# W^T V of a low-rank feed-forward kernel, taken row by row of W, with all loads on SP's queue

## The chip, the cores and the metric

One core of one Trainium2 chip runs the whole program. The metric is device time in microseconds of one execution: 156.87 us, the median of three runs (156.59 to 157.31). TensorE, VectorE, ScalarE, GpSimd and SyncE stand in the profile as PE, DVE, ACT, POOL and SP.

## What is computed

The input x is 2048 tokens (32 x 64) of 1024 numbers. With W 1024 x 1024, eight low-rank experts A (16 x 1024 each) and B (1024 x 16 each), a router Wr (8 x 1024), U (1024 x 256), S (256) and V (1024 x 256):

```
logits = x Wr^T + 5 * onehot(id of the row)         two best experts per token
gates  = softmax of the two best logits
c      = x W^T + 2 * sum_e gate_e * (x A_e^T) B_e^T
out    = x + (c V) * S U^T                          (U * S) V^T applied to c
```

All is fp32. The kernel never forms c: it builds P = W^T V (1024 x 256) once, so that c V = x P + the gated expert part times (B^T V), and multiplies every tile of x by A, Wr and P together.

## The kernel before

**Precision.** Every fp32 operand of a product is split into a high part, rounded to fp32r by a copy on ACT, and a low part, operand minus high part, computed on DVE (for x on POOL). A product is then three matmuls, hi x hi, hi x lo and lo x hi (`triple`, lines 316 to 319).

**The first stage: P = W^T V.** The contraction runs over the 1024 rows of W and V, in eight groups k of 128 rows. The rows of W are loaded in two halves of 512 columns: the first half lies in `vw_raw` beside the 256 columns of V (one transfer of 384 KB for each k), the second half in `w_raw` (one of 256 KB for each k). The stage has sixteen chunks i, one half of W for one k each. Chunk i needs `w_hi` and `w_lo` (a ring of four) and `v_hi`, `v_lo` of its k. On PE a chunk is four column groups of 128 times three matmuls of 256 columns, twelve matmuls (`p_chunk`, line 348); the first is written out in `p_first`. The order before is all eight k of the first half (chunks 0 to 7), then all eight k of the second half (chunks 8 to 15). The eight column groups of P accumulate in four PSUM banks `fin`: banks 0 and 1 are finished after chunk 7, banks 2 and 3 after chunk 15. `split_p` copies a finished bank into `proj_hi` (ACT) and `proj_lo` (DVE).

**What else passes through ACT and DVE in this stage,** in program order, which each engine keeps: the split of A and Wr (`aw_raw`, ACT line 665, DVE line 880) after chunk 12, the split of the first tile of x (ACT line 571, then POOL line 273) after chunk 13, the high part of B (ACT line 673) after chunk 14, and `split_p` of banks 0 and 1 after chunk 11. A wait in one of these holds all that stands behind it on the same engine. `split_w` on ACT waits for the load, and for chunk i - 4 on PE because of the ring.

**Loads.** ACT's queue issues the W parts (all but the first 128 columns) of the first three transfers of V and W; SP's queue issues everything else: the other parts of these three, five whole transfers of V and W, the ids, the eight second halves of W, then A with Wr, the first tile of x transposed, B, the second tile, S, U, and more of x.

**After the stage,** `step(s)` runs over the sixteen tiles of 128 tokens: 24 matmuls of 392 columns on PE for a tile (`project`, line 359), routing on DVE and ACT, and the products with U for pairs of tiles. `step(0)` waits for A, Wr, the first tile and the finished banks of P.

Of the kernel before, what the change touches and what calls it, by code (L numbers as in the profile page):

```python
# [16 lines left out]
def adaln_ffn(nc, xt, x, ids, VW, W, AW, B, U, S, out):  # L17
    P = 128
# [26 lines left out]
    with ExitStack() as ctx:  # L45
# [65 lines left out]
        bv_ps = zt[:, RANK:2 * RANK]  # L111

        vw_load = [sem(f"vw_load{k}") for k in range(OC)]
        vw_rest_load = [sem(f"vw_rest_load{k}") for k in range(3)]
        w_load = [sem(f"w_load{k}") for k in range(OC)]
        aw_load = sem("aw_load")
        b_load = sem("b_load")
# [16 lines left out]
        aw_lo = sem("aw_lo")  # L134
        b_hi_done = sem("b_hi_done")
        b_lo_done = sem("b_lo_done")
        p_hi = sem("p_hi")
        p_lo = sem("p_lo")
        us_hi_done = sem("us_hi_done")
# [42 lines left out]
        bank_a, bank_b, bank_c, bank_d = fin  # L182

        def w_chunk(i):
            return vw_raw[:, i, RANK:RANK + HQ] if i < OC else w_raw[:, i - OC, :]

        block = ctx.enter_context(nc.Block())

# [1 line left out]
        @block.sync  # L190
        def _(sp):
            def load_w(k):
                sp.dma_start(w_raw[:, k, :], W[k, :, :]).then_inc(w_load[k], 16)

            def load_xt(t):
                if t >= XTR:
                    sp.wait_ge(xt_lo, t - XTR + 1)
                sp.dma_start(xt_raw[:, t % XTR, :, :], xt[t, :, :, :]).then_inc(xt_load[t % XTR], 16)

            def load_x(t):  # L200
                if t >= XR:
                    sp.wait_ge(stored[t % XR], 16 * (t // XR))
                sp.dma_start(x_all[:, t % XR, :], x_v[t, :, :]).then_inc(x_load[t % XR], 16)

            def store_head(t):
                sp.wait_ge(end_read, HALF * t + HALF)
                sp.dma_start(out_v[t, :, :], x_all[:, t % XR, :]).then_inc(stored[t % XR], 16)

            def store_pair(p):
                sp.wait_ge(fin_read, READS * (p - 1) + 6)  # L210
                sp.dma_start(out_v[2 * p, :, :], x_all[:, (2 * p) % XR, :]).then_inc(stored[(2 * p) % XR], 16)
                sp.wait_ge(side_add, ADDS * (p - 1) + 3)
                sp.dma_start(out_v[2 * p + 1, :, :], x_all[:, (2 * p + 1) % XR, :]).then_inc(stored[(2 * p + 1) % XR], 16)

            first = RANK + P
            for k in range(3):
                sp.dma_start(vw_raw[:, k, 0:first], VW[k, :, 0:first]).then_inc(vw_load[k], 16)
            for k in range(3, OC):
                sp.dma_start(vw_raw[:, k, :], VW[k, :, :]).then_inc(vw_load[k], 16)
            sp.dma_start(ids_i[:, :], ids).then_inc(ids_load, 16)  # L220
            for k in range(OC):
                load_w(k)
            sp.dma_start(aw_raw[:, :, :], AW).then_inc(aw_load, 16)
            load_xt(0)
            sp.dma_start(b_raw[:, :, :], B).then_inc(b_load, 16)
            load_xt(1)
            sp.dma_start(s_col[:, :], S).then_inc(s_load, 16)
            sp.dma_start(u_raw[:, :, :], U).then_inc(u_load, 16)
            for t in range(2, XTR):
                load_xt(t)  # L230
            for t in range(XR):
                load_x(t)
            for s in range(TILES):
                if s + XTR < TILES:
                    load_xt(s + XTR)
                if s >= 6 and s % 2 == 0:
                    load_x(s)
                    load_x(s + 1)
                if s in (4, 5):
                    store_head(s - 4)  # L240
                if s >= 7 and s % 2 == 1:
                    store_pair((s - 5) // 2)
            p = PAIRS - 2
            sp.wait_ge(fin_read, READS * (p - 1) + 4)
            sp.dma_start(out_v[2 * p, :, 0:BANK], x_all[:, (2 * p) % XR, 0:BANK]).then_inc(stored[(2 * p) % XR], 16)
            sp.wait_ge(fin_read, READS * (p - 1) + 5)
            sp.wait_ge(side_add, ADDS * (p - 1) + 3)
            sp.dma_start(out_v[2 * p + 1, :, :], x_all[:, (2 * p + 1) % XR, :]).then_inc(stored[(2 * p + 1) % XR], 16)
            sp.wait_ge(fin_read, READS * (p - 1) + 6)
            sp.dma_start(out_v[2 * p, :, BANK:D], x_all[:, (2 * p) % XR, BANK:D]).then_inc(stored[(2 * p) % XR], 16)  # L250
            for n in range(5):
                t, lo, hi = ((LAST - 1, 0, BANK), (LAST - 1, BANK, D), (LAST, 0, BANK),
                             (LAST, BANK, BANK + BANK // 2), (LAST, BANK + BANK // 2, D))[n]
                sp.wait_ge(end_read, HEAD_PRODS + n + 1)
                sp.dma_start(out_v[t, :, lo:hi], x_all[:, t % XR, lo:hi]).then_inc(stored[t % XR], 16)
            for j in range(XR):
                n = len(range(j, TILES, XR)) + (2 if j == LAST % XR else 1 if j in ((LAST - 1) % XR, (LAST - 3) % XR) else 0)
                sp.wait_ge(stored[j], 16 * n)
# [56 lines left out]
        def _(pe):  # L315
# [30 lines left out]
                last.then_inc(w_used, 1)  # L346

            def p_chunk(i):
                h, k = divmod(i, OC)
                pe.wait_ge(w_lo_done, i + 1)  # L350
                if h == 0:
                    pe.wait_ge(v_lo_done, k + 1)
                for m in range(MH):
                    cols = slice(m * P, (m + 1) * P)
                    last = triple(p_dst(h, m), w_hi[:, i % WRING, cols], w_lo[:, i % WRING, cols],
                                  v_hi[:, k, :], v_lo[:, k, :], False, True, shared=True)
                last.then_inc(w_used, 1)

            def project(t, k):
                q = t % 2  # L360
# [101 lines left out]
            def step(s, gh_at=1, mix_at=4, z_later=False):  # L462
# [3 lines left out]
                for k in range(DC):  # L466
                    if s == 0 and k == 0:
                        pe.wait_ge(aw_lo, 1)
                        pe.wait_ge(p_lo, 2)
                    if s == 0 and k in (MH, MH + 2):  # L470
                        pe.wait_ge(p_lo, k // 2 + 1)
                    last = project(s, k)
                    if s >= 1 and k == gh_at:
# [68 lines left out]
        @block.scalar  # L542
        def _(act):
            def split_w(i):
                h, k = divmod(i, OC)
                if i == 0:
                    act.wait_ge(vw_rest_load[0], 16)
                    nc.scalar.copy(w_hi[:, 0, P:HQ], w_chunk(0)[:, P:HQ]).then_inc(w_hi_done, 1)
                    return
                if i in (1, 2):  # L550
                    act.wait_ge(vw_rest_load[i], 16)
                if i >= OC:
                    act.wait_ge(w_load[i - OC], 16)
                if i >= WRING:
                    act.wait_ge(w_used, i - WRING + 1)
                nc.scalar.copy(w_hi[:, i % WRING, :], w_chunk(i)).then_inc(w_hi_done, 1)  # L556
# [3 lines left out]
                nc.scalar.copy(v_hi[:, k, :], vw_raw[:, k, 0:RANK]).then_inc(v_hi_done, 1)  # L560

            def split_p(b):
                act.wait_ge(w_used, OC if b < 2 else 2 * OC)
                nc.scalar.copy(proj_hi[:, 2 * b:2 * b + 2, Z0:COLS],
                               fin[b][:, :].rearrange("p (c n) -> p c n", c=2)).then_inc(p_hi, 1)

# [83 lines left out]
                    if s + 2 < TILES:  # L650
                        split_x(s + 2)

            first = RANK + P
            for k in range(3):
                act.dma_start(vw_raw[:, k, first:], VW[k, :, first:]).then_inc(vw_rest_load[k], 16)  # L655
            act.wait_ge(const, 3 + E)
            nc.scalar.activation(esum[:, :], iota_e[:, 0:1], ACT.Exp).then_inc(act_warm, 1)
            act.wait_ge(act_warm, 1)
            for i in range(2 * OC):
                if i < OC:  # L660
                    split_v(i)
                split_w(i)
                if i == OC + 4:
                    act.wait_ge(aw_load, 16)
                    nc.scalar.copy(proj_hi[:, :, 0:Z0], aw_raw[:, :, :]).then_inc(aw_hi, 1)
                if i == OC + 3:
                    split_p(0)
                    split_p(1)
                if i == OC + 5:
                    split_x(0)  # L670
                if i == OC + 6:
                    act.wait_ge(b_load, 16)
                    nc.scalar.copy(b_hi[:, :, :], b_raw[:, :, :]).then_inc(b_hi_done, 1)
            split_p(2)
            split_p(3)
            split_x(1)
            exp_top(0)
            split_x(2)
# [18 lines left out]
        def _(dve):  # L697
# [172 lines left out]
            dve.wait_ge(vw_load[0], 16)  # L870
            nc.vector.tensor_copy(w_hi[:, 0, 0:P], w_chunk(0)[:, 0:P]).then_inc(w_first_hi, 1)
            for i in range(2 * OC):
                if i < OC:
                    split_v(i)
                split_w(i)
                if i == OC:
                    make_target()
                if i == OC + 4:
                    dve.wait_ge(aw_hi, 1)
                    nc.vector.tensor_sub(proj_lo[:, :, 0:Z0], aw_raw[:, :, :],  # L880
                                         proj_hi[:, :, 0:Z0].bitcast(F32)).then_inc(aw_lo, 1)
                if i == OC + 3:
                    split_p(0)
                    split_p(1)
            split_p(2)
            split_p(3)
            dve.wait_ge(b_hi_done, 1)
            nc.vector.tensor_sub(b_lo[:, :, :], b_raw[:, :, :], b_hi[:, :, :].bitcast(F32)).then_inc(b_lo_done, 1)
            dve.wait_ge(setup, 2)
# [66 lines left out]
```

## Time and profile before

| what | value |
|---|---|
| median of three runs | 156.87 us |
| the profiled execution's own time | 156.68 us |
| its span on the core | 154.9 us |
| PE busy | 150.1 us, 97% of the span |
| DVE, POOL, ACT busy | 103.1, 70.1, 65.1 us |
| granted TensorE clock, mean | 1.0 of full speed |
| mean DMA rate over the span | 211 GB/s |

Times in the profile count from the start of the span. A busy figure says how long an engine executed something, not that the end hangs on it. What decides an edit is what each instruction waited for in the stretch that the edit touches; the listing in order of time, read for each engine, shows that.

### The profile page before, as it was taken

The numbers are of one execution on the slowest core, as the hardware profiler recorded it, in microseconds if no ns is written. First come the engines' busy times: TensorE is split into PE (matmuls) and PEld (weight loads), VectorE is DVE, ScalarE is ACT, GpSimd is POOL, SyncE is SP. The second block draws the span as 40 slices with busy tenths as digits, with TensorE's granted clock in tenths as the row PEclk, the third lists the DMA queues.
The fourth block names the chain that finished last, engine by engine and source line by source line (L and its number), as shares of the span: only waits on it lengthen the run. The fifth ranks groups of instructions, "written<-read, shape, count | busy, mean of one in ns | idle before, by whom it ended". The sixth has DMA issues, their size and how long they took to land.

```text
span 154.9 us, 2559 instructions
## 1 busy us (share of the span) xinstructions
PE 150.1 (97%) x883; PEld 139.8 (90%) x883; DVE 103.1 (67%) x299; ACT 65.1 (42%) x147; POOL 70.1 (45%) x53
## 2 busy tenths in 40 slices
PE   7899999999999999999999999999999999999991
PEld 5799999999998999989998999899999989998880
DVE  0698697353658798765578476929692967396861
ACT  4696692519724642551155125414441642233200
POOL 2000024087764741259445935591669068701800
PEclk9999999999999999999999999999999999999999
DMA  5999999995303064148428744854680087006184
GB/s 184 326 395 395 405 418 405 408 402 204 135 7 130 4 271 135 80 154 310 136 99 312 268 135 180 287 215 135 261 259 25 0 292 252 2 22 253 70 333 141
DMA packets 10957, 32.72 MB, mean 211 GB/s; under 512 B 1472, under 2 KB 2496, under 8 KB 10816
## 3 DMA queue, kind: packets, MB, share of 16 engines
q1 hardware_dynamic: 10512, 31.96, 55.9%
q10 hardware_dynamic: 432, 0.59, 1.1%
q8 instruction: 7, 0.11, 0.3%
q14 instruction: 6, 0.05, 0.1%
HBM read 24.16 MB, written 8.39 MB: 210 GB/s over the span
## 4 chain that ended last, share of the span: by engine, by line
PE 93%; DMA 3%; DVE 1%; ACT 0%; ACTq 0%; issue 0%; DVEq 0%
PE pj L317 16%; PE pj L318 16%; PE pj L319 16%; PE fin L317 14%; PE fin L318 13%; PE fin L319 13%; DMA vw_raw<-in_VW 3%; PE zt L384 2%; PE gt L366 1%; PE zt L317 1%; PE zt L319 1%; PE zt L318 1%; DVE w_lo L702 0%; ACT w_hi L556 0%; DVE x_all L831 0%; ACTq L655 0%
## 5 line engine op out<-in xcount | busy, mean ns | idle before, releaser
L273 POOL TENSOR_TENSOR xT_lo<-xt_raw,xT_hi 128x1024 fp32r<-128x1024 f32 x16 | 40.5, 2532 | 55.1 <-ACT xT_hi L571 55.1
L317 PE MATMUL pj<-proj_hi,xT_hi 128*128 128x392 f32 x128 | 44.9, 351 | 0.0
L318 PE MATMUL pj<-proj_lo,xT_hi 128*128 128x392 f32 x128 | 43.5, 340 | 0.0
L319 PE MATMUL pj<-proj_hi,xT_lo 128*128 128x392 f32 x128 | 43.5, 340 | 0.0
L288 POOL TENSOR_TENSOR x_all<-x_all,vw_raw 128x512 f32<-128x512 f32 x18 | 23.0, 1295 | 17.5 <-DVE vw_raw L806 17.5
L317 PE MATMUL fin<-v_hi,w_hi 128*128 128x256 f32 (+1 forms) x84 | 26.9, 321 | 0.5 <-DVE w_lo L702 0.5
L318 PE MATMUL fin<-v_lo,w_hi 128*128 128x256 f32 (+1 forms) x84 | 26.3, 313 | 0.0
L319 PE MATMUL fin<-v_hi,w_lo 128*128 128x256 f32 (+1 forms) x84 | 26.3, 313 | 0.0
L317 PEld LDWEIGHTS pj<-proj_hi,xT_hi 128*128 128x128 f32 x128 | 24.0, 188 | 1.0
L318 PEld LDWEIGHTS pj<-proj_lo,xT_hi 128*128 128x128 f32 x128 | 24.1, 188 | 0.5
L319 PEld LDWEIGHTS pj<-proj_hi,xT_lo 128*128 128x128 f32 x128 | 24.0, 188 | 0.0
L734 DVE SCALAR_TENSOR_TENSOR logit<-target,pj 128x8 f32<-128x8 f32 x16 | 2.6, 161 | 23.3 <-PE pj L319 23.3
L317 PEld LDWEIGHTS fin<-v_hi,w_hi 128*128 128x128 f32 x84 | 16.0, 190 | 1.7 <-DVE w_lo L702 0.9
L319 PEld LDWEIGHTS fin<-v_hi,w_lo 128*128 128x128 f32 x84 | 16.0, 190 | 0.9
L571 ACT CAST xT_hi<-xt_raw 128x1024 fp32r<-128x1024 f32 x16 | 16.8, 1047 | 0.0
L318 PEld LDWEIGHTS fin<-v_lo,w_hi 128*128 128x128 f32 x84 | 16.0, 191 | 0.7
L812 DVE TENSOR_TENSOR x_all<-fin,x_all 128x512 f32<-128x512 f32 x24 | 15.3, 681 | 0.0
L317 PE MATMUL fin<-us_hi,w_hi 128*128 128x512 f32 (+1 forms) x36 | 14.8, 410 | 0.0
L617 ACT CAST ghT_hi<-gt 128x128 fp32r<-128x128 f32 x16 | 4.3, 267 | 22.7 <-PE gt L366 22.7
L319 PE MATMUL fin<-us_hi,w_lo 128*128 128x512 f32 (+1 forms) x36 | 13.7, 380 | 0.0
L318 PE MATMUL fin<-us_lo,w_hi 128*128 128x512 f32 (+1 forms) x36 | 13.7, 380 | 0.0
L625 ACT ACTIVATE etop<-dtop 128x2 f32<-128x2 f32 x16 | 3.3, 203 | 20.9 <-DVE dtop L739 20.9
(87 smaller groups left out, 230.8 us busy)
## 6 DMA issues: line engine op xcount, KB each, us to landing
xt_raw<-in_xt SPq DMA_DIRECT2D x16, 512.0 KB, 3.6
x_all<-in_x SPq DMA_DIRECT2D x16, 512.0 KB, 5.7
out<-x_all SPq DMA_DIRECT2D x13, 512.0 KB, 2.7
w_raw<-in_W SPq DMA_DIRECT2D x8, 256.0 KB, 7.3
vw_raw<-in_VW SPq DMA_DIRECT2D x5, 384.0 KB, 6.8
out<-x_all SPq DMA_DIRECT2D x5, 256.0 KB, 2.0
u_raw<-in_U SPq DMA_DIRECT2D x1, 1024.0 KB, 13.0
vw_raw<-in_VW SPq DMA_DIRECT2D x3, 192.0 KB, 3.3
```

What stands on the lines that cost most here:

```text
L273: nc.gpsimd.tensor_sub(xT_lo[:, t % 2, :, :], xt_raw[:, t % XTR, :, :], xT_hi[:, t % 2, :, :].bitcast(F32)).then_inc(xt_lo, 1)
L288: nc.gpsimd.tensor_add(x_all[:, t % XR, cols], x_all[:, t % XR, cols], ups[:, j, :]).then_inc(side_add, 1)
L317: nc.tensor.matmul(dst, l_hi, r_hi, start=first, stop=False, skip_group_check=shared)
L318: nc.tensor.matmul(dst, l_hi, r_lo, start=False, stop=False, skip_group_check=shared)
L319: return nc.tensor.matmul(dst, l_lo, r_hi, start=False, stop=last, skip_group_check=shared)
L366: nc.tensor.transpose(gt[:, 0:P], gh[:, :], ident[:, :]).then_inc(gt_done, 1)
L384: last = nc.tensor.transpose(zt[:, c + m * P:c + (m + 1) * P], z_sb[:, m * P:(m + 1) * P], ident[:, :])
L571: nc.scalar.copy(xT_hi[:, t % 2, :, :], xt_raw[:, t % XTR, :, :]).then_inc(xt_hi, 1)
L617: nc.scalar.copy(ghT_hi[:, :], gt[:, 0:P]).then_inc(gt_hi, 1)
L625: nc.scalar.activation(etop[:, :], dtop[:, :], ACT.Exp, accum_out=esum[:, :]).then_inc(exp_done, 1)
L734: nc.vector.scalar_tensor_tensor(logit[:, :], target[:, s, :], LANG_BIAS, pj[q][:, LOG:LOG + E], ALU.mult, ALU.add).then_inc(gate_step, 1)
L812: nc.vector.tensor_add(x_all[:, t % XR, cols], src[:, :], x_all[:, t % XR, cols]).then_inc(fin_read, 1)
```

## The change

The chunks of the first stage are taken in the order k = 0 first half, k = 0 second half, k = 1 first half, and so on, so that each V is used for two chunks in a row. The loads follow this order, and all are issued by SP: the first 384 columns of k = 0, the rest of it, the second half of W for k = 0, then for each k the transfer of 384 KB and that of 256 KB, with the ids after k = 2. ACT issues none. All four banks of P now finish in the last two chunks, each with a signal of its own (`p_ready`), and `split_p` of all four follows the loop. The split of A and Wr stands after chunk 10 (12 before), that of the first tile after chunk 12 (13 before), that of B after chunk 13 (14 before). `step(0)` waits for bank k/2 before each second k. The numbers of matmuls, copies and subtractions and the bytes loaded are unchanged; the loads of k = 1 and 2 are one transfer each and no longer two.

```diff
-            for k in range(3):
-                sp.dma_start(vw_raw[:, k, 0:first], VW[k, :, 0:first]).then_inc(vw_load[k], 16)
-            for k in range(3, OC):
+            sp.dma_start(vw_raw[:, 0, 0:first], VW[0, :, 0:first]).then_inc(vw_load[0], 16)
+            sp.dma_start(vw_raw[:, 0, first:], VW[0, :, first:]).then_inc(vw_rest_load, 16)
+            load_w(0)
+            for k in range(1, OC):
                 sp.dma_start(vw_raw[:, k, :], VW[k, :, :]).then_inc(vw_load[k], 16)
-            sp.dma_start(ids_i[:, :], ids).then_inc(ids_load, 16)
-            for k in range(OC):
                 load_w(k)
+                if k == 2:
+                    sp.dma_start(ids_i[:, :], ids).then_inc(ids_load, 16)
...
             def p_chunk(i):
-                h, k = divmod(i, OC)
+                k, h = divmod(i, 2)
...
+                    if k == OC - 1 and m % 2 == 1:
+                        last.then_inc(p_ready, 1)
+                if k < OC - 1:
+                    last.then_inc(w_used, 1)
...
-                        pe.wait_ge(p_lo, 2)
-                    if s == 0 and k in (MH, MH + 2):
+                    if s == 0 and k % 2 == 0:
                         pe.wait_ge(p_lo, k // 2 + 1)
...
             def split_p(b):
-                act.wait_ge(w_used, OC if b < 2 else 2 * OC)
+                act.wait_ge(p_ready, b + 1)
...
-            first = RANK + P
-            for k in range(3):
-                act.dma_start(vw_raw[:, k, first:], VW[k, :, first:]).then_inc(vw_rest_load[k], 16)
...
             for i in range(2 * OC):
-                if i < OC:
-                    split_v(i)
+                if i % 2 == 0:
+                    split_v(i // 2)
                 split_w(i)
-                if i == OC + 4:
+                if i == OC + 2:
                     act.wait_ge(aw_load, 16)
                     nc.scalar.copy(proj_hi[:, :, 0:Z0], aw_raw[:, :, :]).then_inc(aw_hi, 1)
-                if i == OC + 3:
-                    split_p(0)
-                    split_p(1)
+                if i == OC + 4:
+                    split_x(0)
                 if i == OC + 5:
-                    split_x(0)
-                if i == OC + 6:
                     act.wait_ge(b_load, 16)
                     nc.scalar.copy(b_hi[:, :, :], b_raw[:, :, :]).then_inc(b_hi_done, 1)
-            split_p(2)
-            split_p(3)
+            for b in range(FINS):
+                split_p(b)
```

DVE's loop changes in the same way: `split_v(i // 2)` at even i, the low part of A and Wr after chunk 10, and the four `split_p` behind the loop.

## Rows read from the trace of the kernel before

**Rows 1.** The page: busy time of engines, and the chain that ended last.

```profile
PE 150.1 (97%) x883; PEld 139.8 (90%) x883; DVE 103.1 (67%) x299; ACT 65.1 (42%) x147; POOL 70.1 (45%) x53
PE 93%; DMA 3%; DVE 1%; ACT 0%; ACTq 0%; issue 0%; DVEq 0%
```

**Rows 2.** Timeline of PE: start us, us, engine, line, operation, out<-in, count, [idle before <-releaser].

```profile
5.80 0.64 PE L344 MATMUL fin<-v_hi,w_lo 128*128 128x256 f32 x4
6.90 0.39 PE L317 MATMUL fin<-v_hi,w_hi 128*128 128x256 f32 x1 [0.46 <-DVE w_lo L702]
...
8.57 0.38 PE L317 MATMUL fin<-v_hi,w_hi 128*128 128x256 f32 x1
8.80 0.28 PE L318 MATMUL fin<-v_lo,w_hi 128*128 128x256 f32 x1
...
28.70 0.28 PE L319 MATMUL fin<-v_hi,w_lo 128*128 128x256 f32 x1
28.82 0.34 PE L317 MATMUL pj<-proj_hi,xT_hi 128*128 128x392 f32 x1
29.00 0.34 PE L318 MATMUL pj<-proj_lo,xT_hi 128*128 128x392 f32 x1
```

**Rows 3.** Timeline of ACT, same columns.

```profile
5.50 0.62 ACT L556 CAST w_hi<-vw_raw 128x512 fp32r<-128x512 f32 x1 [0.57 <-DMA vw_raw<-in_VW]
6.87 0.41 ACT L560 CAST v_hi<-vw_raw 128x256 fp32r<-128x256 f32 x1 [0.75 <-DMA vw_raw<-in_VW]
7.18 0.62 ACT L556 CAST w_hi<-vw_raw 128x512 fp32r<-128x512 f32 x1
...
13.23 0.62 ACT L556 CAST w_hi<-w_raw 128x512 fp32r<-128x512 f32 x1 [0.44 <-PE fin L319]
...
19.56 1.11 ACT L665 CAST proj_hi<-aw_raw 128x1088 fp32r<-128x1088 f32 x1
20.56 0.62 ACT L556 CAST w_hi<-w_raw 128x512 fp32r<-128x512 f32 x1
21.08 1.05 ACT L571 CAST xT_hi<-xt_raw 128x1024 fp32r<-128x1024 f32 x1
...
29.02 1.08 ACT L564 CAST proj_hi<-fin 128x512 fp32r<-128x512 f32 x2 [4.90 <-PE fin L319]
```

**Rows 4.** Timeline of DVE, same columns.

```profile
6.15 0.69 DVE L702 TENSOR_TENSOR w_lo<-vw_raw,w_hi 128x512 fp32r<-128x512 f32 x1 [0.54 <-ACT w_hi L556]
...
9.53 0.42 DVE L707 TENSOR_TENSOR v_lo<-vw_raw,v_hi 128x256 fp32r<-128x256 f32 x1
...
20.70 1.29 DVE L880 TENSOR_TENSOR proj_lo<-aw_raw,proj_hi 128x1088 fp32r<-128x1088 f32 x1
...
22.68 2.73 DVE L702 TENSOR_TENSOR w_lo<-w_raw,w_hi 128x512 fp32r<-128x512 f32 x1
...
29.64 1.29 DVE L711 TENSOR_TENSOR proj_lo<-fin,proj_hi 128x512 fp32r<-128x512 f32 x2 [3.63 <-ACT proj_hi L564]
```

**Rows 5.** Timeline of POOL, same columns.

```profile
22.22 2.64 POOL L273 TENSOR_TENSOR xT_lo<-xt_raw,xT_hi 128x1024 fp32r<-128x1024 f32 x1 [20.33 <-ACT xT_hi L571]
```

**Rows 6.** Timeline of SP's queue: issue of the load of A and Wr.

```profile
10.00 0.44 SPq L223 DMA_DIRECT2D aw_raw<-in_AW  x1
```

**Rows 7.** DMA issues: out<-in, queue, count, KB each, us from issue to landing.

```profile
aw_raw<-in_AW SPq DMA_DIRECT2D x1, 544.0 KB, 8.8
xt_raw<-in_xt SPq DMA_DIRECT2D x1, 512.0 KB, 10.1
```

**Rows 8.** By stretch: its us; busy PE, PEld, DVE, ACT, POOL; PEclk, DMA share, GB/s.

```profile
2.00:7.00 5.00, 4.54 (x19) 3.41 (x17) 2.37 (x5) 3.46 (x7) 0.00 (x0) 1.00 0.95 324
5.00:6.00 1.00, 1.00 (x9) 1.00 (x9) 0.61 (x2) 0.50 (x1) 0.00 (x0) 1.00 0.77 270
7.00:8.00 1.00, 1.00 (x9) 1.00 (x10) 0.60 (x2) 0.84 (x3) 0.00 (x0) 1.00 1.03 402
```

**Rows 9.** Waits from 28 to 60 us, those of PE: who <- whom: us, times, longest.

```profile
PEld fin L317 <- DVE us_lo L717: 0.4, 1, 0.4
```

More of the change, by code:

```diff
@@ L113, in adaln_ffn @@
         vw_load = [sem(f"vw_load{k}") for k in range(OC)]
-        vw_rest_load = [sem(f"vw_rest_load{k}") for k in range(3)]
+        vw_rest_load = sem("vw_rest_load")
         w_load = [sem(f"w_load{k}") for k in range(OC)]
@@ L136, in adaln_ffn @@
         b_lo_done = sem("b_lo_done")
+        p_ready = sem("p_ready")
         p_hi = sem("p_hi")
@@ L184, in w_chunk @@
         def w_chunk(i):
-            return vw_raw[:, i, RANK:RANK + HQ] if i < OC else w_raw[:, i - OC, :]
+            return vw_raw[:, i // 2, RANK:RANK + HQ] if i % 2 == 0 else w_raw[:, i // 2, :]
         block = ctx.enter_context(nc.Block())
@@ L356, in p_chunk @@
                                   v_hi[:, k, :], v_lo[:, k, :], False, True, shared=True)
-                last.then_inc(w_used, 1)
+                    if k == OC - 1 and m % 2 == 1:
+                        last.then_inc(p_ready, 1)
+                if k < OC - 1:
+                    last.then_inc(w_used, 1)
             def project(t, k):
@@ L544, in split_w @@
             def split_w(i):
-                h, k = divmod(i, OC)
+                k, h = divmod(i, 2)
                 if i == 0:
-                    act.wait_ge(vw_rest_load[0], 16)
+                    act.wait_ge(vw_rest_load, 16)
                     nc.scalar.copy(w_hi[:, 0, P:HQ], w_chunk(0)[:, P:HQ]).then_inc(w_hi_done, 1)
                     return
[L550 to L553, printed above, removed]
+                if h == 1:
+                    act.wait_ge(w_load[k], 16)
                 if i >= WRING:
@@ L872, in _ @@
             for i in range(2 * OC):
-                if i < OC:
-                    split_v(i)
+                if i % 2 == 0:
+                    split_v(i // 2)
                 split_w(i)
@@ L877, in _ @@
                     make_target()
-                if i == OC + 4:
+                if i == OC + 2:
                     dve.wait_ge(aw_hi, 1)
@@ L881, in _ @@
                                          proj_hi[:, :, 0:Z0].bitcast(F32)).then_inc(aw_lo, 1)
[L882 to L886, printed above, removed]
+            for b in range(FINS):
+                split_p(b)
             dve.wait_ge(b_hi_done, 1)
```

## The prediction

> **What bounds the kernel now.** I read the page's busy times and its chain first: PE is busy 97% of the span and holds 93% of the chain [rows 1], so the time moves by what PE stands still, and by nothing else. The edit touches only the stage that builds P, so next I read PE in order of time there. Chunk 0 ends its last group with matmuls that start at 5.80 and last 0.64; chunk 1 starts at 6.90 after 0.46 of idle put down to `w_lo`; chunk 2 starts at 8.57, and from 8.80 a matmul starts every 0.12 us up to 28.70; the first matmul of `step(0)` starts at 28.82 [rows 2]. After that PE has one wait of note up to 60 us, 0.4 us [rows 9]. I call 28.82 T: all behind it hangs on PE and on chains that start from it, so what T moves, the end moves. The stage's stalls lie only ahead of 8.80, and their cause is in ACT's timeline: `w_hi` of chunk 1 starts at 5.50 after 0.57 of waiting for a DMA, `v_hi` of k = 2 at 6.87 after 0.75 of it [rows 3]. Later in the stage PE is the bound and the splits run ahead of it: `w_hi` of chunk 8 waits for PE at 13.23 [rows 3].
>
> **What the change gives at the front.** Chunk 0 needs the same first 384 KB. Chunk 1 then needs 640 KB in all, where before it needed the second transfer pair (768 KB, with parts of the third in between); chunk 2 needs 1024 KB, before 1152. At the mean 324 GB/s of 2 to 7 us [rows 8] the 128 KB saved are about 0.4 us for each. With `w_hi` of chunk 1 at about 4.5 (5.50 before less 1.0, as 128 KB less and no third pair shares the engines), `w_lo` is done near 5.8 and PE goes on at the end of chunk 0, at about 6.3: 0.6 saved. Chunk 2 follows at 7.75 by PE's own pace, with its splits just ready: V of k = 1 by about 6.0, then 0.31 to the next copy, 0.62, and 0.69 on DVE [rows 3, 4] give 7.7. Against 8.57 that is 0.8 us. Ends: 0 if the transfers come no sooner, 0.8. I take 0.8, but below it turns out not to matter.
>
> **What the change adds: the wait for A and Wr.** Before, ACT came to the split of A and Wr at 19.56 [rows 3]; the load had landed at 10.00 + 8.8 = 18.8 [rows 6, 7], so nothing waited. Now it stands behind `w_hi` of chunk 10. By PE's pace (12 x 0.12 = 1.445 us a chunk with the small start) chunk 7 starts at 7.75 + 5 x 1.445 = 15.0, `w_hi` of chunk 10 follows 0.3 later, as that of chunk 8 followed chunk 5 (28.82 - 11 x 1.445 = 12.9; 13.23), and ACT is at the wait by 15.9, long before the load. The load stands in the same place of the byte order: V, W, ids and A are 5672 KB before it has landed, before and after. So its landing, L, can move only by the rate. In 2 to 7 us the core moved 5 x 324 = 1620 KB, against 5 x 402 = 2010 at the pace of 7 to 8 us [rows 8]; the lack of 390 KB is 0.97 us. The new order makes two of the small pairs whole transfers and leaves one queue. Ends: nothing recovered, L = 18.8; all recovered, L = 17.8. I take the middle, L = 18.3, as no row speaks for either end.
>
> What is queued behind this wait on ACT: `w_hi` of chunk 11, V of k = 6, `w_hi` of 12, x, `w_hi` of 13. On DVE the low part of A stands ahead of `w_lo` of chunk 11. Step by step from X = L + 0.03 (0.03 taken for ACT to start after a landing): ACT's copy to DVE's subtraction 20.70 - 19.56 = 1.14; that one lasts 1.29, the next starts 0.08 before its recorded end; `w_lo` 0.69; PE 0.06 later, as 6.15 + 0.69 to 6.90 [rows 2 to 4]. Chunk 11 starts at X + 3.10 = 21.43. Free of the wait it would start at 7.75 + 9 x 1.445 = 20.8; before, it started at 28.82 - 5 x 1.445 = 21.6. So the wait takes 0.65 back, and the gain in front could be 0.65 smaller without showing.
>
> **The second stall: POOL's subtraction of x.** Before, `w_lo` of chunk 14 took 2.73 instead of 0.69: it started at 22.68, inside POOL's `xT_lo` of 22.22 to 24.86, and ended at 25.41, 0.55 after POOL [rows 4, 5]. Chunk 14 was due only at 25.9, so it was hidden. Now the order is `w_hi` 11, V 6, `w_hi` 12, x. From X: 1.00 to `w_hi` 11, 0.52 to V, 0.31 to `w_hi` 12, 0.52 to x, all start to start (20.56 to 21.08 for the two 0.52, 6.87 to 7.18 for the 0.31) [rows 3]; x's load lands at 18.8 + 1.74 before (10.48 issued, 10.1), L + 1.7 after, in time. So x is copied from X + 2.35, lasts 1.05, POOL follows 0.09 later at X + 3.49 = 21.82 and ends 2.64 later at 24.46. DVE comes to `w_lo` of chunk 13 at X + 4.1 (1.14 + 1.21 (that is 1.29 - 0.08), and 0.69, 0.42 and 0.69 less an overlap of some 0.1 for `w_lo` 11, V and `w_lo` 12 [rows 4]), inside POOL's operation, and ends it at 24.46 + 0.55 = 25.01. PE starts chunk 13 at 25.07; free of that it would at 21.43 + 0.11 + 24 x 0.12 = 24.4. Cost 0.65. Ends: 0, if DVE is not held; 1.2, if POOL is itself held by `w_lo` 12 up to its end. I take the 0.65 of the rows, since the place in time is like that of before. Behind it `w_lo` 14 and 15 are ready about 0.6 ahead of PE.
>
> **The end of the stage.** 36 matmuls follow chunk 13's start: T = 25.07 + 0.11 + 36 x 0.12 = 29.50, against 28.82: +0.68 us.
>
> **The four banks.** `split_p` of banks 0 and 1 no longer runs at 18 us but at the end. Two banks take ACT 1.08 and DVE 1.29; ACT started 0.20 after T on the third [rows 2 to 4]. Bank 0 is complete 18 matmuls before T (2.16), bank 1 12, bank 2 6, bank 3 0. ACT follows at T - 1.96, - 1.24, - 0.52, + 0.20, and `proj_lo` is ready 1.25 after each: T - 0.7, 0.0, + 0.7, + 1.45. `step(0)` wants them at T, T + 1.08, + 2.16, + 3.24 (six matmuls 0.18 apart for two k [rows 2]). All are covered, the first by 0.7 us; if that cover went, each us would count in full. The next x split on ACT comes sooner than before, B's likewise: nothing waits for either. SP's queue takes over one issue of ACT's net (18 issues ahead of A, 17 before) at 0.44 each; the bytes it feeds take longer than that, so it costs nothing. Sum: 0.68, made on the profiled execution (156.68, span 154.9): 157.36. The median of the runs is 0.19 above that execution, so 157.55.
>
> **A rule on the queues.** The share of the DMA engines in 5 to 6 us is 0.77 while two queues hand over [rows 8]; one may read that as a cost of two queues. The Trainium skill, "DMA: Bandwidth & Descriptors", section "Issuing engines are not separate DMA queues", says that transfers of all issuing engines run on the same 16 DMA engines and that several issuers save only issue time. By it, giving up ACT's queue wins no rate; that is the second rival below, whose time needs no page.
>
> **The rivals.**
> First: the gain in front stays. T = 7.75 + 0.11 + 168 x 0.12 = 28.02, -0.80: 156.1. It needs the load of A and Wr by 20.8 - 3.13 = 17.65 for chunk 11, and by 7.75 + 11 x 1.445 - 6.77 = 16.9 for chunk 13 where POOL holds DVE. For it: the front stalls are real. Against it: even the full pace gives 17.8.
> Second, slower: no rate comes back, and L = 18.8. The mechanism is the same wait with its price in full: each 0.1 later is 0.1 on T, through both stalls. T = 30.0, +1.18: 158.05. From L = 18.4 on, it is slower by over 0.5%. For it: the queue is saturated from 7 us on whoever issues, and the slow stretch of 2 to 7 us may belong to the start, not to the queues. Against it: the small transfers of 192 KB, two of three pairs of which go.
> Third: DVE is not held by POOL. T = 21.43 + 0.11 + 60 x 0.12 = 28.74, -0.08: 156.8. Against it is the 2.73 of the row.
> The change may also fail to bring the front forward; then T is the forecast's still, as the slack of 0.65 says.
>
> **How the numbers follow.** This kernel's measurement tells about 0.5%, 0.78 us. Forecast (L from 17.8 to 18.4, both stalls, +0.2 to +0.78): 0.45. Second rival (+0.78 to +1.5): 0.41. First: 0.07. Third: 0.07. So faster 0.07, same 0.45 + 0.07 = 0.52, slower 0.41. The predicted time is 157.55. Range: down to 156.6, which leaves out the first rival; up to 158.3, with POOL held 0.25 more atop the second.
>
> **What would show it.** Right: chunk 1 of PE with no idle ahead of it; an ACT copy of A and Wr just after its load's landing near 18.3, with over 2 us of idle put down to that DMA; PE idle near 21 and near 24.5, the second behind a `w_lo` of over 2 us; T near 29.5. Wrong: that load landing by 17.6; a `w_lo` of chunk 13 of 0.69; PE waiting for `proj_lo` at T; or a difference that arises behind T.

## The result, and the profile after

The changed kernel is slower: 159.22 us, median of four runs (158.61 to 159.64), against 156.78 of the kernel before; ratio 1.0129, 95% interval 1.0084 to 1.0174. Measured a second time it was 1.0106 (1.0071 to 1.0141). The forecast was 157.55 in a range up to 158.3: the direction of the sum was right, the size was not. The four runs of before lie low: beside the experiments below, 19 to 30 runs of it had medians of 157.23 to 157.34, so each ratio is to be read against the runs measured beside it.

The profiled execution took 159.18, its span is 157.4 (before 156.68 and 154.9). First the page: busy times and the chain.

```profile
PE 150.3 (95%) x883; PEld 139.7 (89%) x883; DVE 103.3 (66%) x299; ACT 65.4 (42%) x147; POOL 70.3 (45%) x53
PE 81%; DMA 6%; SPq 6%; DVE 4%; ACT 1%; issue 1%; DVEq 0%
```

PE does the same 883 matmuls in nearly the same busy time as in [rows 1], but its share of the chain fell from 93% to 81%. What stands there now is a load. The chain in order of time (start us, us, what) shows it whole:

```profile
9.82 0.43 SPq L194
10.26 0.04 issue
10.30 9.41 DMA aw_raw<-in_AW
19.71 0.02 issue
19.73 1.11 ACT proj_hi L664
20.84 0.02 issue
20.87 1.29 DVE proj_lo L876
22.16 0.60 DVE w_lo L698
22.76 0.34 DVE v_lo L703
23.10 3.43 DVE w_lo L698 x2
26.53 0.04 issue
26.57 0.38 PE fin L319
```

From the start of the span to 19.71 the chain is SP issuing transfers and the last of them, A with Wr, being on its way; then ACT's high part, DVE's low part, `w_lo` of chunk 11, V of k = 6, and `w_lo` of chunks 12 and 13. PE in order of time, its starts after idle and the first matmul of `step(0)`:

```profile
6.58 0.38 PE L319 MATMUL fin<-v_hi,w_hi 128*128 128x256 f32 x1 [0.81 <-DVE w_lo L698]
...
8.89 0.39 PE L319 MATMUL fin<-v_hi,w_hi 128*128 128x256 f32 x1 [0.61 <-DVE w_lo L698]
...
22.82 0.38 PE L319 MATMUL fin<-v_hi,w_hi 128*128 128x256 f32 x1 [0.72 <-DVE w_lo L698]
...
26.57 0.38 PE L319 MATMUL fin<-v_hi,w_hi 128*128 128x256 f32 x1 [0.63 <-DVE w_lo L698]
...
30.98 0.34 PE L319 MATMUL pj<-proj_hi,xT_hi 128*128 128x392 f32 x1
```

These are the starts of chunks 1, 2, 11 and 13; against [rows 2] chunk 1 is 0.32 earlier, chunk 2 is 0.32 later, and T, the start of `step(0)`, is 30.98 against 28.82: +2.16 of the +2.50 between the two executions. Behind T the two move apart by a further 0.34. That is a difference of executions and not of the change: from T to the end of the span it is 126.1 to 126.4 us in all thirteen profiles of this document, and a version below with T 0.08 earlier than before had a span 0.2 longer. The engines that make the two late stalls, ACT, DVE and POOL in order of time:

```profile
19.73 1.11 ACT L664 CAST proj_hi<-aw_raw 128x1088 fp32r<-128x1088 f32 x1 [2.73 <-DMA aw_raw<-in_AW]
22.09 1.04 ACT L573 CAST xT_hi<-xt_raw 128x1024 fp32r<-128x1024 f32 x1
```

```profile
20.87 1.29 DVE L876 TENSOR_TENSOR proj_lo<-aw_raw,proj_hi 128x1088 fp32r<-128x1088 f32 x1 [3.15 <-ACT proj_hi L664]
23.68 2.83 DVE L698 TENSOR_TENSOR w_lo<-w_raw,w_hi 128x512 fp32r<-128x512 f32 x1
```

```profile
23.21 2.76 POOL L275 TENSOR_TENSOR xT_lo<-xt_raw,xT_hi 128x1024 fp32r<-128x1024 f32 x1 [21.32 <-ACT xT_hi L573]
```

ACT stood 2.73 us at the load that it never waited for before [rows 3]; the `w_lo` of chunk 13 took 2.83 us while POOL ran, 23.21 to 25.97, as that of chunk 14 had [rows 4, 5]. The Trainium skill, "SBUF — State Buffer", section "Who interferes with whom", says that a DVE instruction with two SBUF inputs contends with a POOL instruction that reads SBUF, for a shared pair of ports that acts as an exclusive lock; the trace agrees, 2.83 us against 0.69 alone. Last, the DMA rate, same columns as [rows 8]:

```profile
2.00:7.00 5.00, 4.19 (x21) 3.37 (x20) 2.04 (x4) 1.75 (x5) 0.00 (x0) 1.00 0.87 294
```

294 GB/s where it was 324: the forecast had expected this rate to rise.

### The profile page after: what moved, and what is told of

It reads as the page before. It is cut to its first block, busy times and chain, and to the rows that moved or that the text cites. A ratio compares the mean times of both kernels' runs of the same rounds, so it can differ in the third digit from the quotient of the medians.

```text
span 157.4 us, 2555 instructions
## 1 busy us (share of the span) xinstructions
PE 150.3 (95%) x883; PEld 139.7 (89%) x883; DVE 103.3 (66%) x299; ACT 65.4 (42%) x147; POOL 70.3 (45%) x53
## 4 chain that ended last, share of the span: by engine, by line
PE 81%; DMA 6%; SPq 6%; DVE 4%; ACT 1%; issue 1%; DVEq 0%
PE pj L319 16%; PE pj L321 16%; PE pj L320 16%; PE fin L319 10%; PE fin L321 9%; PE fin L320 9%; DMA aw_raw<-in_AW 6%; DVE w_lo L698 3%; SPq L194 2%; SPq L221 2%; PE zt L389 2%; PE gt L371 1%; DVE proj_lo L876 1%; ACT proj_hi L664 1%; PE zt L319 1%
## 5 line engine op out<-in xcount | busy, mean ns | idle before, releaser
L627 ACT ACTIVATE etop<-dtop 128x2 f32<-128x2 f32 x16 | 3.3, 204 | 21.1 <-DVE dtop L735 21.1
```

What stands on the lines that cost most here:

```text
L627: nc.scalar.activation(etop[:, :], dtop[:, :], ACT.Exp, accum_out=esum[:, :]).then_inc(exp_done, 1)
```

## The experiments

The theory after the result: with L the landing of A and Wr, T = L + 11.2 through the two stalls, and L went from 18.8 to 19.7 because one queue feeds the DMA engines too slowly at the start (called Q below). Its rivals: the durations of the moved splits or the late splits of P cost the time; and, for L, the order and sizes of the transfers (O).

**The splits back at their old places** (A and Wr after chunk 12, x after 13, B after 14; the loads stay as changed).

```diff
-                if i == OC + 2:
+                if i == OC + 4:
                     act.wait_ge(aw_load, 16)
...
-                if i == OC + 4:
+                if i == OC + 5:
                     split_x(0)
-                if i == OC + 5:
+                if i == OC + 6:
                     act.wait_ge(b_load, 16)
```

> The changed kernel with the splits of A and Wr, x and B at their old places again (after chunks 12, 13, 14). Theory (the landing of A and Wr at 19.7 gates PE through what is queued behind its wait): both later stalls of PE go, chunks 3 to 15 run without a gap from the start of chunk 2 at 8.9, and the first matmul of step(0) starts at 8.89 + 0.11 + 168 x 0.12 = 29.2, against 31.0 in the changed kernel and 28.8 before; time about 0.4 us over the kernel before, 157.2. Rival (the time went into the late splits of the four banks, or into what lies behind step(0)): step(0) at 29.2 as well, but the time stays near 159.

Measured: 157.15 us, ratio 1.0004 (0.9974 to 1.0033): no difference from the kernel before can be told. ACT, DVE and PE of its profile:

```profile
19.93 1.10 ACT L664 CAST proj_hi<-aw_raw 128x1088 fp32r<-128x1088 f32 x1 [0.77 <-DMA aw_raw<-in_AW]
```

```profile
22.87 2.63 DVE L703 TENSOR_TENSOR v_lo<-vw_raw,v_hi 128x256 fp32r<-128x256 f32 x1
```

```profile
26.16 0.39 PE L319 MATMUL fin<-v_hi,w_hi 128*128 128x256 f32 x1 [0.46 <-DVE w_lo L698]
29.13 0.34 PE L319 MATMUL pj<-proj_hi,xT_hi 128*128 128x392 f32 x1
```

The load lands as late as in the changed kernel (19.9), but two more chunks stand ahead of its wait, and T is 29.13 for an expected 29.2. The new order of chunks, the four late splits of P and the single queue are all still in: together they cost nothing measurable against the kernel before. (That is a sum; the last experiment suggests that it hides a small gain and a small loss.) One expectation missed: a stall of 0.46 remained, at chunk 14, since POOL now held the V split ahead of its `w_lo`. The front was faster in this execution, chunk 2 at 8.24 and not 8.89, which makes up for it; so the agreement of T with its expectation is in part luck.

**The second stall alone:** x and B split behind chunk 15's copy.

```diff
-                if i == OC + 4:
+                if i == OC + 7:
                     split_x(0)
-                if i == OC + 5:
                     act.wait_ge(b_load, 16)
```

> The changed kernel with only the splits of x and B moved behind chunk 15's on ACT, so that POOL's subtraction of x runs when DVE has done its w_lo. Theory: the first stall stays (chunk 11 at 22.8), the second goes, no w_lo lasts over 0.7; step(0) at 22.82 + 0.11 + 60 x 0.12 = 30.1 instead of 31.0. Rival (the second stall is ACT's or DVE's backlog, not POOL's hold on DVE): chunk 13 is still late and step(0) near 31.0.

PE of its profile:

```profile
22.92 0.39 PE L319 MATMUL fin<-v_hi,w_hi 128*128 128x256 f32 x1 [1.14 <-DVE w_lo L697]
...
30.22 0.34 PE L319 MATMUL pj<-proj_hi,xT_hi 128*128 128x392 f32 x1
```

The first stall stayed, no other followed, and T was 30.22 for 30.1; with L = 19.8 that is L + 10.4. So POOL's hold on DVE costs 0.9 of the 11.3 between L and T. The time was 158.39 us, of a single execution.

**The load of A and Wr behind the first tile of x.**

```diff
-            sp.dma_start(aw_raw[:, :, :], AW).then_inc(aw_load, 16)
             load_xt(0)
+            sp.dma_start(aw_raw[:, :, :], AW).then_inc(aw_load, 16)
```

> The changed kernel with the load of A and Wr issued behind that of the first tile of x, so that it lands some 1.3 us later (512 KB at 400 GB/s), near 21.0. Theory: step(0) is its landing plus 11.2, 32.2, 1.3 us later than in the changed kernel. Rival (the durations of the splits count, not the wait for the load): step(0) stays at 31.0.

T moved with the load, but further than expected: L = 21.1, T = 32.88, L + 11.8; 161.03 us, of a single execution. PE, and the stretches around its stall:

```profile
24.17 0.58 PE L319 MATMUL fin<-v_hi,w_hi 128*128 128x256 f32 x1 [2.44 <-DVE w_lo L698]
...
32.88 0.34 PE L319 MATMUL pj<-proj_hi,xT_hi 128*128 128x392 f32 x1
```

```profile
23.00:24.00 1.00, 0.00 (x0) 0.00 (x0) 1.00 (x2) 1.00 (x3) 0.00 (x0) 1.00 0.97 401
24.00:25.00 1.00, 0.83 (x4) 0.83 (x5) 1.00 (x3) 1.00 (x3) 0.43 (x1) 0.51 0.99 406
25.00:26.00 1.00, 1.00 (x6) 1.00 (x6) 1.00 (x2) 1.00 (x3) 1.00 (x1) 0.50 1.04 414
26.00:27.00 1.00, 1.00 (x7) 1.00 (x6) 1.00 (x1) 0.78 (x2) 1.00 (x1) 0.50 1.01 401
27.00:28.00 1.00, 1.00 (x9) 1.00 (x9) 1.00 (x2) 0.62 (x1) 0.29 (x1) 0.79 1.02 406
```

After 2.44 us of idle the granted clock is 0.5 of full speed, the 1.2 GHz level, until past 27 us, and the matmuls start 0.21 us apart instead of 0.12. The stall has a second price, behind itself.

**The load of A and Wr ahead of those of k = 6 and 7.**

```diff
                 if k == 2:
                     sp.dma_start(ids_i[:, :], ids).then_inc(ids_load, 16)
-            sp.dma_start(aw_raw[:, :, :], AW).then_inc(aw_load, 16)
+                if k == 5:
+                    sp.dma_start(aw_raw[:, :, :], AW).then_inc(aw_load, 16)
```

> The changed kernel with the load of A and Wr issued ahead of the loads of k = 6 and 7 (1280 KB), so that it lands near 16.5, when ACT reaches its wait at 17.0. Theory: no stall at chunk 11. The second stall then hangs on the load of x alone (landing 21.0): ACT waits for it, POOL's subtraction runs from 22.1 to 24.8, w_lo of chunk 13 ends near 25.4 against 24.85 when it is due; step(0) at 29.9; about 1.0 us over before. Rival: as above, step(0) stays near 31.0, or the loads of k = 6 and 7, 1.4 us later, become the bound.

158.02 us, ratio 1.0061 (1.0032 to 1.0091): slower than before by 0.7 us between the medians, 1.0 by the ratio, for an expected 1.0; about half of the changed kernel's loss is gone. The load landed at 8.53 + 7.8 = 16.3, as expected; ACT came to its split of A and Wr at 18.81 and waited for no load there. T was 31.04 in the profiled execution, for an expected 29.9, and that is the rival's number; but this execution took 159.21, one of the slowest of the ten, and its T comes from the front, as PE has no idle of note behind chunk 1. So the trace doesn't confirm the expected T, and the medians alone speak for it. In the front the second half of W for k = 0 came late, chunk 1 started at 7.86 after 1.73 of idle, and the clock fell to 0.5 for 9 to 11 us:

```profile
7.86 0.39 PE L320 MATMUL fin<-v_hi,w_hi 128*128 128x256 f32 x1 [1.73 <-DVE w_lo L699]
```

```profile
8.00:9.00 1.00, 1.00 (x7) 1.00 (x8) 0.75 (x2) 1.00 (x3) 0.00 (x0) 0.67 0.95 358
9.00:10.00 1.00, 1.00 (x7) 1.00 (x7) 1.00 (x3) 0.87 (x3) 0.00 (x0) 0.50 1.05 403
10.00:11.00 1.00, 1.00 (x6) 1.00 (x6) 0.94 (x2) 0.73 (x2) 0.00 (x0) 0.50 1.03 387
```

**Three loads back on ACT's queue,** all else as changed.

```diff
             sp.dma_start(vw_raw[:, 0, 0:first], VW[0, :, 0:first]).then_inc(vw_load[0], 16)
-            sp.dma_start(vw_raw[:, 0, first:], VW[0, :, first:]).then_inc(vw_rest_load, 16)
-            load_w(0)
             for k in range(1, OC):
                 sp.dma_start(vw_raw[:, k, :], VW[k, :, :]).then_inc(vw_load[k], 16)
-                load_w(k)
+                if k >= 2:
+                    load_w(k)
...
+            act.dma_start(vw_raw[:, 0, RANK + P:], VW[0, :, RANK + P:]).then_inc(vw_rest_load, 16)
+            for k in range(2):
+                act.dma_start(w_raw[:, k, :], W[k, :, :]).then_inc(w_load[k], 16)
```

> The changed kernel with three loads given back to ACT's queue (the rest of k = 0 and the second halves of W of k = 0 and 1), the order of chunks and the splits as changed. The load of A and Wr has landed by 19.7 in the changed kernel and by 18.8 before. Theory Q (one queue feeds the DMA engines too slowly at the start): the rate of 2 to 7 us comes back from 294 to about 324 GB/s, the load lands near 18.9, step(0) starts 11.2 later at 30.1; time 0.9 us below the changed kernel. Theory O (the order and the sizes of the transfers do it): rate, landing and step(0) stay at 294 GB/s, 19.7 and 31.0.

Rate of 2 to 7 us, and PE:

```profile
2.00:7.00 5.00, 5.00 (x19) 3.94 (x17) 2.13 (x5) 3.74 (x7) 0.00 (x0) 1.00 1.00 366
```

```profile
22.31 0.39 PE L318 MATMUL fin<-v_hi,w_hi 128*128 128x256 f32 x1 [0.69 <-DVE w_lo L700]
...
26.07 0.39 PE L318 MATMUL fin<-v_hi,w_hi 128*128 128x256 f32 x1 [0.63 <-DVE w_lo L700]
...
30.48 0.34 PE L318 MATMUL pj<-proj_hi,xT_hi 128*128 128x392 f32 x1
```

366 GB/s, more than the 324 expected; L = 19.2 instead of 18.9 all the same, and T = L + 11.3. 157.97 us, ratio 1.0043 (1.0015 to 1.0070), where the changed kernel had 1.0129 and 1.0106. Of the 1.25 us between the medians, 0.5 stands in the T of the two profiles; the profiled execution, 158.42, is among the slower ones of this version.

**The kernel before with its three ACT loads on SP's queue.**

```diff
             for k in range(3):
                 sp.dma_start(vw_raw[:, k, 0:first], VW[k, :, 0:first]).then_inc(vw_load[k], 16)
+                sp.dma_start(vw_raw[:, k, first:], VW[k, :, first:]).then_inc(vw_rest_load[k], 16)
...
-            for k in range(3):
-                act.dma_start(vw_raw[:, k, first:], VW[k, :, first:]).then_inc(vw_rest_load[k], 16)
```

> The kernel before with the three loads of ACT's queue issued by SP instead, each behind its partner; nothing else. Theory Q: rate of 2 to 7 us near 295 GB/s, A and Wr landed near 19.7, the old places of the splits hide most of it (ACT comes there at 19.6); chunk 2 on PE some 0.3 to 0.5 later than 8.57 and step(0) at 29.1 to 29.3, time +0.3 to +0.5 us. Theory O: rate 324, landing 18.8, time within 0.2 us of before.

```profile
2.00:7.00 5.00, 4.54 (x18) 3.74 (x16) 1.97 (x5) 2.38 (x7) 0.00 (x0) 1.00 0.91 282
```

The old order with one queue has the low rate too, 282 GB/s; the load lands at 11.35 + 8.7 = 20.0, T = 29.34 for an expected 29.1 to 29.3; 157.51 us, ratio 1.0026 (0.9999 to 1.0052), a loss of the expected size whose interval still includes no difference. Here SP issues the load 1.35 us later than before, so this run alone can't tell the rate from the issue time.

**The small transfers of k = 1 and 2 on SP's queue.**

```diff
+                if k <= 2:
+                    sp.dma_start(vw_raw[:, k, 0:first], VW[k, :, 0:first]).then_inc(vw_load[k], 16)
+                    sp.dma_start(vw_raw[:, k, first:], VW[k, :, first:]).then_inc(vw_more[k - 1], 16)
+                else:
+                    sp.dma_start(vw_raw[:, k, :], VW[k, :, :]).then_inc(vw_load[k], 16)
```

> The changed kernel with the loads of k = 1 and 2 in two transfers of 192 KB each, as before, but on SP's queue. Theory Q: no better than the changed kernel, A and Wr land at 19.7 or later (two more issues). Theory O (the larger transfers start slowly): the rate of 2 to 7 us comes back to about 324 GB/s and the landing to 18.9.

305 GB/s, L = 20.7, T = 32.56 (again with a stall of over 2 us, 2.31, and the clock down behind it), 160.58 us, of a single execution: small transfers don't bring the landing back. With the two runs before it, Theory O falls.

**One load on ACT's queue,** the second half of W for k = 0.

```diff
-            load_w(0)
...
+            act.dma_start(w_raw[:, 0, :], W[0, :, :]).then_inc(w_load[0], 16)
```

> The changed kernel with one load only, the second half of W for k = 0, on ACT's queue. If two queues feed the engines sooner at the start (Theory Q), already this one brings the rate of 2 to 7 us to 310 or more (one queue gave 282 to 305) and that load in before 4.9 instead of 5.2; if only the number of loads taken off SP's queue matters, it stays at 295 to 305.

```profile
2.00:7.00 5.00, 4.75 (x15) 3.45 (x14) 2.37 (x5) 2.96 (x7) 0.00 (x0) 1.00 0.97 343
```

```profile
18.73 1.10 ACT L664 CAST proj_hi<-aw_raw 128x1088 fp32r<-128x1088 f32 x1 [0.89 <-DMA aw_raw<-in_AW]
```

343 GB/s for an expected 310 or more, and that second half landed at 0.73 + 3.4 = 4.1, before the 4.9 expected: a single transfer on the second queue already brings the rate up. L = 18.7 and T = 29.98; 158.19 us, of a single execution. This T is L + 11.3 by chance. PE has no stall at chunk 11 or 13 here; its lateness comes from the front:

```profile
7.69 0.41 PE L318 MATMUL fin<-v_hi,w_hi 128*128 128x256 f32 x1
```

Chunk 1 starts at 7.69 and chunk 2 at 9.83, since up to 9.18 the matmuls start 0.21 us apart (a record of 0.41 us and not 0.28), although the granted clock reads 1.00 in these rows; from 9.83 it is fourteen chunks without a gap to 29.98. ACT's 0.89 us at the load is hidden, with 0.1 us to spare at chunk 13.

**The changed kernel again.**

> The changed kernel itself, unaltered, beside the next one on one chip. Expected: ratio to before 1.010 to 1.013, with A and Wr landing near 19.7 in the profile and step(0) 11.3 later; if the landing varies between executions, step(0) follows it at the same distance.

L = 19.9, T = 31.19: the same 11.3. 159.25 us, ratio 1.0106. SP issued the load at 9.82, sooner than the 10.00 of before, and it landed 1.1 us later: the later landing is not issue time.

**Both mended:** three loads on ACT's queue as above, splits at their old places as above; measured twice.

> The changed kernel with both: the three loads on ACT's queue and the splits of A, x and B at their old places. The candidate for a version ahead of both. If Theory Q holds, chunk 1 starts near 6.3 and chunk 2 near 8.0, no later stall; step(0) at 8.0 + 0.11 + 168 x 0.12 = 28.3, 0.5 us ahead of before: ratio 0.997. If Theory O holds, the front is that of the changed kernel: step(0) at 29.2, ratio 1.002.

> The version with three loads on ACT's queue and the splits at their old places, once more: ratio to before 0.996 to 0.998 if the gain of the first measurement is real, 1.000 if it was that chip's. Against the changed kernel 0.985.

Rate and T of the first, T of the second:

```profile
2.00:7.00 5.00, 4.91 (x18) 3.55 (x16) 2.04 (x5) 3.65 (x7) 0.00 (x0) 1.00 1.01 375
```

```profile
28.74 0.34 PE L318 MATMUL pj<-proj_hi,xT_hi 128*128 128x392 f32 x1
```

```profile
28.70 0.34 PE L318 MATMUL pj<-proj_hi,xT_hi 128*128 128x392 f32 x1
```

156.62 us, ratio 0.9965 (0.9947 to 0.9984), and 156.64 us, ratio 0.9961 (0.9934 to 0.9987): ahead of both kernels, by 0.4% of the one before. T was expected at 28.3; chunk 2 starts at 8.58, no sooner than before, because the second half of W for k = 0 still landed only at 5.63 (1.16 + 4.47). Against the profiled execution of before T gains only 0.1. That one was near the lower end of its runs (156.68; the 30 runs beside these had a median of 157.23), so where the 0.6 us between the medians lies isn't shown. Against the version with only the splits moved back (1.0004, 0.9974 to 1.0033), which differs by the three loads alone, the intervals just overlap: a price of some 0.4% for the single queue with the splits in their old places is likely, not shown.

## Why the prediction was wrong

**The step that failed is the size of L,** the landing of A and Wr: 18.3 in the sum, 19.71 measured. "Ends: nothing recovered, L = 18.8; all recovered, L = 17.8" left out that the rate could fall, and it fell, from 324 to 294 GB/s. With the measured L the prediction's own sum gives T = 30.9; measured 30.98. So 1.41 of the error of T, 30.98 - 29.50 = 1.48, is that of L. The profiled execution missed its sum by 159.18 - 157.36 = 1.82: this 1.48, and the 0.34 behind T. In the three profiles where both late stalls stand and the granted clock stays at full speed:

| run | L | T | T - L |
|---|---|---|---|
| three loads on ACT's queue | 19.21 | 30.48 | 11.27 |
| changed kernel | 19.71 | 30.98 | 11.27 |
| changed kernel, again | 19.91 | 31.19 | 11.28 |

L here is the start of ACT's copy less 0.02. The wait as cause is shown: where it holds PE, T moves with L one for one, and moving the wait behind two more chunks removes the loss.

**Right:** both late stalls, their places and their causes (chunk 11 at X + 3.1 for measured 3.09; the `w_lo` of chunk 13 held by POOL, 2.83 us, with 0.63 of idle on PE for a forecast 0.65); the four late splits of P, for which PE never waits at T; that the front doesn't matter while L decides; that little arises behind T.

**Wrong in the front:** chunk 1 was expected at 6.3 and came at 6.58, chunk 2 at 7.75 and came at 8.89. Fewer bytes were needed, but they came more slowly. Chunk 2 was 1.14 late, more than the slack of 0.65 that the text gave the front; it didn't show because the late load still left PE idle for 0.72 and 0.63 behind it. In the repeated run chunk 2 came at 8.21.

**The statement on the queue.** "SP's queue takes over one issue of ACT's net ... so it costs nothing" was wrong: it counted issue time only. With one queue, 2 to 7 us ran at 282 to 305 GB/s in eight profiles and L was 19.7 to 20.7 wherever that load kept its place; with at least one early load on ACT's queue it ran at 324 to 375 in five, and L was 17.7 to 19.2. The gap is clearest from 3 to 4 us, 192 to 246 GB/s against 355 to 414; the kernel before, the changed one, its repeat, and the one with three loads on ACT's queue:

```profile
3.00:4.00 1.00, 1.00 (x4) 0.52 (x2) 0.23 (x1) 0.96 (x4) 0.00 (x0) 1.00 0.98 355
3.00:4.00 1.00, 1.00 (x4) 0.80 (x3) 0.53 (x2) 0.74 (x2) 0.00 (x0) 1.00 0.70 214
3.00:4.00 1.00, 1.00 (x4) 0.81 (x3) 0.56 (x2) 0.76 (x2) 0.00 (x0) 1.00 0.98 239
3.00:4.00 1.00, 1.00 (x4) 0.52 (x2) 0.23 (x1) 0.89 (x3) 0.00 (x0) 1.00 1.02 393
```

The rule of the Trainium skill ("DMA: Bandwidth & Descriptors", "Issuing engines are not separate DMA queues"), that several issuers save only issue time, gives no reason for such a gap. At the start the traces go against it; from 12 to 17 us they show 399 to 412 GB/s in all thirteen profiles, but by then SP alone issues in each of them. Why one queue starts more slowly is not shown. "Feeds too slowly" is only a name for it: in the repeated run the DMA engines were busy 0.98 of the time from 3 to 4 us and still moved 239 GB/s. Nor was it separated from what moves along with it: with all loads on SP's queue ACT loads its activation table at 0.73 us, beside the first transfers, and at 1.16 or 2.13 where it issues loads first. Nor is the rate of 2 to 7 us all of L, as 366 GB/s went with 19.2 and 375 with 17.7; the same kernel, both mended, had L = 17.7 and 19.0 in its two profiles.

## What to carry to other kernels

A load that an in-order engine waits for gates all that stands behind it, so an edit that moves its consumer by two chunks can cost more than the stalls it was made for: compare the consumer's new time with the load's landing before anything else, and give the landing a range on both sides. If the first loads of a kernel are on the path, try them on two issuing queues and compare the rate of the first microseconds: here it rose from 282 to 324 GB/s in the old order and from 294 to 366 in the new one. And look at what POOL and DVE share when a split of x moves: a hold of over 2 us was free in one place and 0.9 us on the path in another.

## What the runs showed of the hardware

TensorE's clock fell behind a stall. It was at 0.5 of full speed (1.2 GHz) for about 3.4 us behind idle stretches of 1.73, 2.44 and 2.31 us, and stayed at full speed (2.4 GHz) behind those of 0.72, 1.14 and 1.59 in the changed kernel, the second experiment and the repeated run. Behind the 2.44 and 2.31, T - L was 11.8 and 11.9 instead of 11.3, a cost of 0.5 to 0.6 us. The early loads vary: the second half of W for k = 0 landed between 5.0 and 6.4 us in seven profiles of kernels that have it third in one queue, and PE's idle ahead of chunk 1 was 0.31 and 0.81 us where it landed at 5.2, 1.73 where it landed at 6.4.
